# In two graph passes, a third of the table look-ups is replaced by GpSimd gathers weighed on ScalarE

## The chip, the cores and the metric

The kernel runs on one core of a Trainium2 chip. The metric is the device time of one execution, in microseconds (us). Engines are called TensorE (PE in the profile, its weight loads PEld), VectorE (DVE), ScalarE (ACT), GpSimd (POOL) and SyncE (SP, which here only issues transfers).

## The reference, cut to what matters

A graph of 3125 nodes (64 values each) and 100000 edges passes through four layers. The change touches the last, a signed graph convolution that is applied twice. With weights split by sign, each application is a sum over edges:

```
wp, wn = where(w >= 0, w, 0), where(w < 0, -w, 0)
def gcn(x, w):                     # for wp and for wn, with a weight matrix and bias each
    dinv = rsqrt(segment_sum(w, dst) + 1)
    agg  = segment_sum((x @ W.T)[src] * (dinv[src] * w * dinv[dst]), dst)
    return agg + (x @ W.T) * dinv**2 + b
h   = relu(gcn(x, wp) - gcn(x, wn))
out = relu(gcn(h, wp) - gcn(h, wn))
```

So for each edge a row of its source node is taken, multiplied by the edge's two weights (positive and negative part, 64 values each, 128 in all), and added to its target node.

## The kernel before, in words

Nodes are kept in 25 tiles (`NT`) of 125 nodes, one node per partition. Edges have been sorted into slots of 128: 36 bins of target nodes, three bins (`SLOTS = 3`) handled at a time, for each of the 25 source tiles. One source tile with its three bins is a chunk; there are 12 x 25 = 300 chunks (`NCHUNK`), in an order that is fixed in the program. Edges that find no slot are "left over" and are done in a loop behind each pass.

`edge_pass` is called three times: for "edges" (an earlier layer), "near" and "far" (the two applications of the signed convolution, line tags `sp_` and `sq_`). In near and far, chunk c goes like this:

- SyncE loads `hot_src` (a 128 x 384 one-hot matrix, three slots of 128 columns, bf16) from DRAM into a ring of eight buffers (`load_hot`, line 2292).
- TensorE looks up the source rows (`look_up`, line 1599): for each of three slots, three matmuls with the one-hot slot as weights and the node table as moving operand. The table is split into three bf16 pieces, so that the sum is exact in f32; it has 66 columns in near (64 values and two scales) and 128 in far. Nine matmuls fill one PSUM bank. Look-ups run three chunks ahead (`LOOK_AHEAD`).
- VectorE makes `hot_dst` (line 1417, here "the target": which row of a bin each edge goes to, 128 x 270), in near multiplies the two looked-up scales with the edge weights (`weigh`, line 1425, "the weights"), and multiplies the looked-up rows by them into `msg` (line 1450, "the message", 128 x 384).
- TensorE sums messages by target (`add_up`, line 1611): three f32 matmuls, 90 x 128 each, which the trace shows as six weight loads and six matmuls. They accumulate over 25 chunks.
- ScalarE copies the sums out once in 25 chunks (`evacuate`, line 1557), and SyncE stores the result.

Every step waits on semaphores that count chunks (`rows_taken`, `dst_made`, `looked_up`, `added`), so that an engine runs ahead by the number of its buffers: four for messages and targets, six PSUM banks for look-ups. At the start of near, ScalarE also computes `k.table` = x times the two scales (`far_terms`, line 2536, 50 activations), which is used only behind the pass. GpSimd issues one gather of left-over rows per pass (line 1382) and then waits.

An earlier pass, `relation_pass` (`rp_`), already takes the third slot of most chunks by a GpSimd gather (line 1783) in place of a look-up.

Of the kernel before, what the change touches and what calls it, by code (L numbers as in the profile page):

```python
# [14 lines left out]
P = 128  # L15
# [156 lines left out]
class Program:  # L172
    def __init__(self, nc, ctx, dram):
# [41 lines left out]
        self.near_rows = dram_rows("near_rows", NPAD, D + 2)  # L215
        self.far_rows = dram_rows("far_rows", NPAD, H)
        self.hot_rows = nc.dram_tensor("hot_rows", (NCHUNK, P, SLOTS * P), BF16, kind="Internal").ap()

# [1031 lines left out]


def edge_pass(k, tag, kind, pieces, table, width, cols, sem, ring, aside=None, act_aside=None):

# [9 lines left out]
    DST_SLOTS, MSG_SLOTS, SUM_SLOTS, HOT_SLOTS = 4, 4, 3, Ring.HOT_SLOTS  # L1263
    edges = kind == "edges"
    KEY_BANKS = 2 if edges else 0
    ROW_BANKS = 6 - KEY_BANKS
    slots = lambda a, c: a[:, c * SLOTS:(c + 1) * SLOTS]
    with ExitStack() as ctx:
# [6 lines left out]
        fence, weighed, squared = sem("fence"), sem("weighed"), sem("squared")  # L1275
        hot_io, hot_src = ring.hot_io, ring.hot_src

        found = FIELD if edges else width
# [40 lines left out]
        with nc.Block() as block:  # L1319
# [56 lines left out]
            @block.gpsimd  # L1376
            def _(pool):
                if aside:
                    aside(nc.gpsimd)
                ring.wait_rows(pool)  # L1380
                pool.wait_ge(left_idx, 1)
                pool.indirect_dma_start(left_row[:, :], None, table,
                                        bass.IndirectOffsetOnAxis(left_no[:, 0:1], 0)).then_inc(left_rows, 16)
                left_count = pool.value_load(k.left_tiles[0:1, 0:1], min_val=1, max_val=EPAD // P)
                with pool.Fori(0, left_count) as i:
                    pool.wait_ge(left_idx, i + 2)
                    pool.sem_inc(fence, 1)
                    pool.indirect_dma_start(left_row[:, :], None, table,
                                            bass.IndirectOffsetOnAxis(left_no[:, 0:1], 0)).then_inc(left_rows, 16)
                    pool.wait_ge(left_rows, i * 16 + 32)  # L1390
                    pool.sem_inc(fence, 1)

            @block.vector
            def _(dve):
# [26 lines left out]
                def weigh(c):  # L1421
                    got = looked(c)
                    if c >= MSG_SLOTS:
                        dve.wait_ge(rows_taken, c - MSG_SLOTS + 1)
                    v.tensor_tensor(factor[:, c % MSG_SLOTS, :, :], got[:, :, D:D + 2], slots(k.slot_w, c), ALU.mult)\
                        .then_inc(weighed, 1)
# [5 lines left out]
                def message(c):  # L1432
# [15 lines left out]
                    else:  # L1448
                        by, x = slots(k.slot_w, c), got.rearrange("p s (a f) -> p s a f", a=2)
                    v.tensor_tensor(to, x, by.unsqueeze(3).broadcast_to([P, SLOTS, 2, D]), ALU.mult)\  # L1450
                        .then_inc(rows_taken, 1)

# [77 lines left out]
            def _(act):  # L1530
# [22 lines left out]
                def evacuate(j):  # L1553
# [3 lines left out]
                    nc.scalar.activation(totals[:, j % 2, :, :], sum_bank(j), ACT.Copy).then_inc(evacuated, 1)  # L1557

                nc.scalar.preload_act_table(ACT.Copy)
                if act_aside:  # L1560
                    act_aside(nc.scalar)
                for c in range(-SPELL_AHEAD, NCHUNK):
                    ahead = c + SPELL_AHEAD - 1
                    if edges and c >= 0:
                        rectify(c)
                    if edges and 0 <= ahead < NCHUNK:
                        square_key(ahead)
                    if edges and 0 <= ahead - 1 < NCHUNK:
                        hot_source(ahead - 1)
                    if c % NT == 1 and c > NT:  # L1570
                        evacuate(c // NT - 1)
# [6 lines left out]
            def _(pe):  # L1578
# [10 lines left out]
                def look_up(c):  # L1589
# [5 lines left out]
                    if c >= ROW_BANKS:  # L1595
                        pe.wait_ge(rows_taken, c - ROW_BANKS + 1)
                    for s in range(SLOTS):
                        for piece in range(3):
# [5 lines left out]
                def add_up(c):  # L1604
                    j, i = c // NT, c % NT
                    pe.wait_ge(dst_made, c + 1)
                    pe.wait_ge(msg_made if edges else rows_taken, c + 1)
                    if i == 0 and j >= 2:
                        pe.wait_ge(evacuated, j - 1)
# [890 lines left out]
def program(nc, dram, out):  # L2500
    with ExitStack() as ctx:
# [27 lines left out]
        with nc.sbuf_tensor("near_pieces", [P, NT, 3, D + 2], BF16) as pieces, ExitStack() as held, semaphores(nc, "sp") as sem:  # L2529
            ring = Ring(k, held, sem, "sp")  # L2530
            near_table(k, pieces, sem, ring)

            def far_terms(act):
                for t in range(NT):
                    for j in range(2):
                        act.activation(k.table[:, t, j * D:(j + 1) * D], k.x[:, t, :], ACT.Copy, scale=k.dinv[:, t, j:j + 1])

            edge_pass(k, "sp", "near", pieces, k.near_rows, D + 2, H, sem, ring, act_aside=far_terms)
        with nc.sbuf_tensor("far_pieces", [P, NT, 3, H], BF16) as pieces, ExitStack() as held, semaphores(nc, "sq") as sem:
            ring = Ring(k, held, sem, "sq")  # L2540
            gcn_mid(k, pieces, sem, ring)
# [58 lines left out]
```

## Time and profile before

| | us |
|---|---|
| median of 3 runs | 3882.38 |
| lowest and highest run | 3877.11, 3891.0 |
| profiled execution, its time | 3880.98 |
| profiled execution, span from first to last instruction | 3879.3 |
| near, first look-up to last message | 3102.9 to 3399.7 |
| far, first look-up to last message | 3462.6 to 3816.7 |

Over the span TensorE is busy 75%, VectorE 77%, ScalarE 36%, GpSimd 31%. These shares are means over stages with different limits; the two passes that the change touches are to be read from their own stretches.

### The profile page before, as it was taken

The numbers are of one execution on the slowest core, as the hardware profiler recorded it, in microseconds if no ns is written. First come the engines' busy times: TensorE is split into PE (matmuls) and PEld (weight loads), VectorE is DVE, ScalarE is ACT, GpSimd is POOL, SyncE is SP. The second block draws the span as 40 slices with busy tenths as digits, with TensorE's granted clock in tenths as the row PEclk, the third lists the DMA queues.
The fourth block names the chain that finished last, engine by engine and source line by source line (L and its number), as shares of the span: only waits on it lengthen the run. The fifth ranks groups of instructions, "written<-read, shape, count | busy, mean of one in ns | idle before, by whom it ended". The sixth has DMA issues, their size and how long they took to land. (4 is left out here: it accounts for less than half of the span.)

```text
span 3879.3 us, 77817 instructions
## 1 busy us (share of the span) xinstructions
PE 2903.3 (75%) x25843; PEld 2103.0 (54%) x25926; DVE 2985.1 (77%) x6871; ACT 1393.6 (36%) x2725; POOL 1210.0 (31%) x1109
## 2 busy tenths in 40 slices
PE   0158888888407707707769999699999699979994
PEld 0135555555302202202259999456565499969994
DVE  6877777778589999999977777555555599968887
ACT  0024444444304405405459999233333210010000
POOL 0034445455238737636600000155555100000000
PEclk9998888889659959959979999799999799989997
DMA  7936565556458828728847675122222144323331
GB/s 304 378 98 179 147 182 163 166 161 182 148 162 289 260 83 283 253 88 277 258 157 219 216 230 168 47 66 69 66 65 66 37 107 108 106 55 89 91 90 37
DMA packets 444431, 596.30 MB, mean 154 GB/s; under 512 B 82795, under 2 KB 331434, under 8 KB 444052
## 3 DMA queue, kind: packets, MB, share of 16 engines
q1 hardware_dynamic: 395623, 450.37, 39.4%
q0 software_dynamic: 34592, 68.90, 5.9%
q10 hardware_dynamic: 13836, 72.12, 4.8%
q8 instruction: 220, 3.60, 0.4%
q14 instruction: 160, 1.30, 0.1%
HBM read 354.68 MB, written 230.75 MB: 151 GB/s over the span
## 5 line engine op out<-in xcount | busy, mean ns | idle before, releaser
L1213 PE MATMUL psum<-a_probs,z 128*65 128x512 f32 (+1 forms) x1050 | 436.3, 555 | 134.1 <-DVE a_probs L1111 133.4
L914 POOL DMA_INDIRECT slots<-bc_rec,idx x400 | 392.1, 980 | 399.8 <-ACT bc_rec L874 300.8
L1806 DVE TENSOR_SCALAR rp_hot_dst<-rp_ramp,slot_key 128x696 bf16<-128x696 f16 x900 | 298.8, 401 | 230.3 <-PE psum L1950 230.3
L535 POOL DMA_INDIRECT slots<-h,idx x256 | 336.7, 1315 | 310.8 <-DMA h<-recs 239.8
L1147 ACT ACTIVATE a_tops<-a_tops,a_s_low 128x512 f32<-128x512 f32 (+2 forms) x300 | 283.0, 946 | 271.8 <-DVE a_tops L1102 254.7
L1213 PEld LDWEIGHTS psum<-a_probs,z 128*65 128x65 f32 x1050 | 122.5, 139 | 443.5 <-DVE a_probs L1111 275.3
L1783 POOL DMA_INDIRECT rp_fetch<-piece_rows,slot_row x283 | 279.2, 987 | 247.5 <-PE psum L1950 191.1
L1102 DVE SCALAR_TENSOR_TENSOR a_tops<-table,a_s_rest,big 128x512 f32<-128x512 f32 (+2 forms) x300 | 307.7, 1028 | 2.8 <-DMA big<-shift_rows 2.8
L1111 DVE SCALAR_TENSOR_TENSOR a_probs<-a_tops,a_counts 128x512 f32<-128x512 f32 (+2 forms) x300 | 289.8, 967 | 11.4 <-ACT a_tops L1147 7.6
L1878 ACT ACTIVATE rp_msg<-psum 128x192 bf16<-128x192 f32 (+1 forms) x456 | 176.2, 387 | 310.3 <-PE psum L1924 275.6
L793 PE MATMUL psum<-acc 128*128 128x512 f16 x1000 | 194.1, 339 | 115.3 <-issue 64.2
L1611 PE MATMUL psum<-sp_msg,sp_hot_dst 128*90 128x128 f32 x1800 | 260.2, 281 | 0.0
L1611 PE MATMUL psum<-ep_msg,ep_hot_dst 128*90 128x131 f32 x1800 | 257.2, 278 | 3.3 <-ACT ep_msg L1535 3.1
L1611 PE MATMUL psum<-sq_msg,sq_hot_dst 128*90 128x128 f32 x1800 | 252.2, 277 | 0.0
L762 DVE TENSOR_SCALAR acc<-bc_ramp,bc_key_s,bc_base_s 128x625 f16<-128x625 f16 x500 | 245.9, 492 | 6.0 <-issue 6.0
L1941 PE MATMUL psum<-rp_hot_dst,rp_msg 128*128 128x184 bf16 (+1 forms) x1151 | 239.9, 307 | 10.2 <-DVE rp_hot_dst L1806 2.0
L1204 PE MATMUL psum<-ident,a_shifts 128*10 128x128 f32 x15 | 5.7, 377 | 283.6 <-DVE a_shifts L1096 266.3
L1599 PE MATMUL psum<-edge_pieces,ep_hot_src 128*128 128x131 bf16 x2700 | 209.8, 222 | 0.8 <-ACT ep_hot_src L1550 0.7
L1438 DVE TENSOR_TENSOR ep_sums<-psum,ep_rec 128x393 f32<-128x393 f32 x300 | 169.8, 566 | 52.5 <-PE psum L1599 49.8
L1611 PEld LDWEIGHTS psum<-ep_msg,ep_hot_dst 128*90 128x90 f32 x1800 | 206.6, 158 | 5.8 <-DVE ep_hot_dst L1417 5.7
L1599 PE MATMUL psum<-far_pieces,sq_hot_src 128*128 128x128 bf16 x2700 | 200.7, 220 | 5.2 <-PEq L2077 5.2
L1611 PEld LDWEIGHTS psum<-sp_msg,sp_hot_dst 128*90 128x90 f32 x1800 | 203.1, 159 | 0.0
(452 smaller groups left out, 6613.7 us busy)
## 6 DMA issues: line engine op xcount, KB each, us to landing
slots<-big ACTq DMA_DIRECT2D x60, 1012.5 KB
ep_rec<-slots SPq DMA_DIRECT2D x60, 1012.5 KB, 6.0
a_counts<-edge_counts SPq DMA_DIRECT2D x75, 538.5 KB
a_counts<-edge_counts SPq DMA_DIRECT2D x150, 256.0 KB
a_counts<-edge_counts SPq DMA_DIRECT2D x75, 512.0 KB
edge_counts<-bc_counts SPq DMA_DIRECT2D x12, 3125.0 KB
hot_rows<-ep_hot_src SPq DMA_DIRECT2D x300, 96.0 KB
sp_hot_src<-hot_rows SPq DMA_DIRECT2D x300, 96.0 KB
```

Of the source, the lines that this page charges most:

```text
L535: pool.indirect_dma_start(k.slots, bass.IndirectOffsetOnAxis(k.idx[:, at:at + 1], 0), self.rows[y][:, t, :], None).then_inc(self.scattered ...
L762: last = v.tensor_scalar(to_s[:, u, :], ramp[:, :], column(key_s, t), column(base_s, j), ALU.subtract, ALU.is_equal)
L914: pool.indirect_dma_start(k.slots, bass.IndirectOffsetOnAxis(k.idx[:, first + t:first + t + 1], 0), rec[:, j, t, :], None).then_inc(scatte ...
L1102: v.scalar_tensor_tensor(tops[:, cols], shift_1[:, cols], s_rest[:, s:s + 1], shift_2[:, cols], ALU.add, ALU.max).then_inc(topped, 1)
L1111: v.scalar_tensor_tensor(probs[:, cols], tops[:, cols], 1.0, counts[:, cols], ALU.min, ALU.mult)\
L1147: nc.scalar.activation(tops[:, cols], tops[:, cols], ACT.Exp, bias=s_low[:, s:s + 1])\
L1213: last = nc.tensor.matmul(sums[:, a:b], k.z[:, s, 0:D + 1], probs[:, a:b], start=s == 0, stop=True, skip_group_check=True)
L1599: last = nc.tensor.matmul(got[:, s, :], hot_src[:, c % HOT_SLOTS, s * P:(s + 1) * P], pieces[:, c % NT, piece, :], start=s == 0 and piece ...
L1611: last = nc.tensor.matmul(sum_bank(j)[:, s, :], hot_dst[:, c % DST_SLOTS, s, :], msg[:, c % MSG_SLOTS, s, :], start=i == 0 and s == 0, sto ...
L1783: pool.indirect_dma_start(fetch[:, n % FETCH_SLOTS, :], None, k.piece_rows, bass.IndirectOffsetOnAxis(k.slot_row[:, c:c + 1], 0))\
L1806: v.tensor_scalar(hot_dst[:, q % HOT_SLOTS, :], ramp[:, :], k.slot_key[:, q:q + 1], None, ALU.is_equal)\
L1941: nc.tensor.matmul(sum_bank(s, part), message(q)[:, 0:2 * D], hot_dst[:, q % HOT_SLOTS, a:b], start=starts_bank(q, part), stop=True, skip_ ...
```

## The change

In near and far, chunks with c % 3 other than 2 (from chunk 25 on in near, from 5 on in far: 183 and 196 of 300) are handled differently in their third slot:

- TensorE looks up two slots, not three (six matmuls), and only 256 of the 384 one-hot columns are loaded.
- GpSimd gathers the 128 source rows of the third slot from DRAM by an indirect transfer, 128 f32 values (512 bytes) each, into a ring of six buffers (`fetch`); a buffer is free when ScalarE has used it. In far the rows come from the table in DRAM that is there already (`far_rows`). In near they come from a new one, `term_rows`: a copy of `k.table`, which ScalarE stores once its 50 activations are done, and GpSimd waits for.
- ScalarE multiplies the gathered rows by the edge's two weights, in two activations of 128 x 64, straight into the third slot of `msg`.
- VectorE weighs two slots, not three; the target keeps all three.
- TensorE waits for ScalarE's products (`fetch_taken`) before it sums a fetched chunk.

```diff
+def edge_fetches(kind):
+    first = {"edges": NCHUNK, "near": NT, "far": FIRST_FETCH}[kind]
+    return [c for c in range(first, NCHUNK) if c % 3 != 2]
+
+def looked_columns(kind):
+    return lambda c: (SLOTS - 1 if c in edge_fetches(kind) else SLOTS) * P
...
+    FETCHES = edge_fetches(kind)
+    FETCH_NO, FETCH_SLOTS = {c: n for n, c in enumerate(FETCHES)}, 6
+    looked_slots = lambda c: SLOTS - 1 if c in FETCH_NO else SLOTS
...
             def _(pool):
...
+                if kind == "near":
+                    pool.wait_ge(terms_in, 16)
+                for n, c in enumerate(FETCHES):
+                    if n >= FETCH_SLOTS:
+                        pool.wait_ge(fetch_taken, n - FETCH_SLOTS + 1)
+                    pool.indirect_dma_start(fetch[:, n % FETCH_SLOTS, :], None, k.term_rows if kind == "near" else table,
+                                            bass.IndirectOffsetOnAxis(k.slot_row[:, c:c + 1], 0))\
+                        .then_inc(fetch_in[n % FETCH_SLOTS], 16)
...
-                    v.tensor_tensor(to, x, by.unsqueeze(3).broadcast_to([P, SLOTS, 2, D]), ALU.mult)\
-                        .then_inc(rows_taken, 1)
+                    some = slice(0, looked_slots(c))
+                    v.tensor_tensor(to[:, some], x[:, some], by[:, some].unsqueeze(3).broadcast_to([P, looked_slots(c), 2, D]),
+                                    ALU.mult).then_inc(rows_taken, 1)
...
+                def weigh_fetched(c):
+                    n = FETCH_NO[c]
+                    act.wait_ge(fetch_in[n % FETCH_SLOTS], 16 * (n // FETCH_SLOTS + 1))
+                    if c >= MSG_SLOTS:
+                        act.wait_ge(added, c - MSG_SLOTS + 1)
+                    at = c * SLOTS + SLOTS - 1
+                    for j in range(2):
+                        last = nc.scalar.activation(msg[:, c % MSG_SLOTS, SLOTS - 1, j * D:(j + 1) * D],
+                                                    fetch[:, n % FETCH_SLOTS, j * D:(j + 1) * D], ACT.Copy,
+                                                    scale=k.slot_w[:, at, j:j + 1])
+                    last.then_inc(fetch_taken, 1)
...
                 if act_aside:
-                    act_aside(nc.scalar)
+                    act_aside(nc.scalar).then_inc(terms_made, 1)
+                    act.wait_ge(terms_made, 1)
+                    act.dma_start(k.term_rows.rearrange("(t p) f -> p t f", p=P), k.table[:, :, :]).then_inc(terms_in, 16)
                 for c in range(-SPELL_AHEAD, NCHUNK):
+                    if c in FETCH_NO:
+                        weigh_fetched(c)
...
-                    for s in range(SLOTS):
+                    for s in range(looked_slots(c)):
                         for piece in range(3):
...
                     pe.wait_ge(msg_made if edges else rows_taken, c + 1)
+                    if c in FETCH_NO:
+                        pe.wait_ge(fetch_taken, FETCH_NO[c] + 1)
```

## Rows read from the trace of the kernel before

**Rows 1.** Windows: busy us of PE, PEld, DVE, ACT, POOL; PE clock; DMA share; GB/s
```profile
3200.00:3250.00 50.00, 50.00 (x766) 49.41 (x764) 50.00 (x152) 0.97 (x2) 0.00 (x0) 1.00 0.40 108
...
3600.00:3650.00 50.00, 50.00 (x637) 49.52 (x636) 42.34 (x85) 0.97 (x2) 0.00 (x0) 1.00 0.31 85
```

**Rows 2.** Timeline of near: start, duration (us), engine, line, output, inputs
```profile
3252.40 0.43 PEld L1599 LDWEIGHTS psum<-near_pieces,sp_hot_src 128*128 128x128 bf16 x9
...
3252.59 0.43 DVE L1417 TENSOR_TENSOR sp_hot_dst<-bin_lane,slot_dst 128x270 f32<-128x270 f32 x1
3252.76 0.67 PEld L1611 LDWEIGHTS psum<-sp_msg,sp_hot_dst 128*90 128x90 f32 x6
...
3252.99 0.17 DVE L1425 TENSOR_TENSOR sp_factor<-psum,slot_w 128x6 f32<-128x6 f32 x1
3253.10 0.56 DVE L1450 TENSOR_TENSOR sp_msg<-psum,sp_factor 128x384 f32<-128x384 f32 x1
3253.39 0.43 PEld L1599 LDWEIGHTS psum<-near_pieces,sp_hot_src 128*128 128x128 bf16 x9
```

**Rows 3.** Timeline of far, one chunk of TensorE's weight loads
```profile
3602.54 0.60 PEld L1599 LDWEIGHTS psum<-far_pieces,sq_hot_src 128*128 128x128 bf16 x9
...
3603.10 0.67 PEld L1611 LDWEIGHTS psum<-sq_msg,sq_hot_dst 128*90 128x90 f32 x6
...
3603.72 0.60 PEld L1599 LDWEIGHTS psum<-far_pieces,sq_hot_src 128*128 128x128 bf16 x9
```

**Rows 4.** Windows of 10 ns of the weight loads alone, near, then far
```profile
3252.50:3252.51 0.01, 0.00 (x1) 1.00 0.00 0
...
3602.64:3602.65 0.01, 0.00 (x0) 1.00 1.18 384
```

**Rows 5.** Timeline of the first chunks of near
```profile
3103.72 0.43 DVE L1417 TENSOR_TENSOR sp_hot_dst<-bin_lane,slot_dst 128x270 f32<-128x270 f32 x1
3103.89 1.09 POOL L1382 DMA_INDIRECT sp_left_row<-near_rows,sp_left_no  x1 [37.17 <-DVE sp_left_no L1454]
...
3106.69 0.43 DVE L1417 TENSOR_TENSOR sp_hot_dst<-bin_lane,slot_dst 128x270 f32<-128x270 f32 x1
...
3107.04 0.16 DVE L1425 TENSOR_TENSOR sp_factor<-psum,slot_w 128x6 f32<-128x6 f32 x1
3107.11 0.55 DVE L1450 TENSOR_TENSOR sp_msg<-psum,sp_factor 128x384 f32<-128x384 f32 x1
3107.58 0.43 DVE L1417 TENSOR_TENSOR sp_hot_dst<-bin_lane,slot_dst 128x270 f32<-128x270 f32 x1
```

**Rows 6.** Timeline of ScalarE at the start of near
```profile
3104.20 12.04 ACT L2536 ACTIVATE table<-x,dinv 128x64 f32<-128x64 f32 x50
3130.60 0.49 ACT L1557 ACTIVATE sp_totals<-psum 90x384 f32<-90x384 f32 x1 [14.35 <-PE psum L1611]
```

**Rows 7.** Timeline of GpSimd in the relation pass
```profile
2602.40 0.98 POOL L1783 DMA_INDIRECT rp_fetch<-piece_rows,slot_row  x1 [0.30 <-issue]
```

**Rows 8.** Timeline of the attention stage, GpSimd and VectorE
```profile
1217.45 2.08 POOL L535 DMA_INDIRECT slots<-h,idx  x1 [0.30 <-issue]
1217.46 1.21 DVE L1111 SCALAR_TENSOR_TENSOR a_probs<-a_tops,a_counts 128x1024 f32<-128x1024 f32 x1
...
1218.60 0.74 DVE L1102 SCALAR_TENSOR_TENSOR a_tops<-table,a_s_rest,big 128x512 f32<-128x512 f32 x1
...
1219.83 0.97 POOL L535 DMA_INDIRECT slots<-h,idx  x1 [0.30 <-issue]
1219.86 1.27 DVE L1102 SCALAR_TENSOR_TENSOR a_tops<-table,a_s_rest,big 128x1024 f32<-128x1024 f32 x1
```

**Rows 9.** Timeline of a left-over gather behind near
```profile
3411.18 0.95 POOL L1388 DMA_INDIRECT sp_left_row<-near_rows,sp_left_no  x1 [306.20 <-DVE sp_left_no L1454]
...
3413.87 0.15 DVE L1476 TENSOR_TENSOR sp_left_out<-sp_left_row,sp_left_rec 128x2 f32<-128x2 f32 x1
```

**Rows 10.** Window behind the far table's last store, columns as in rows 1
```profile
3458.00:3462.00 4.00, 0.00 (x0) 0.00 (x0) 3.86 (x6) 2.21 (x3) 0.00 (x0) 0.61 0.31 82
```

More of the change, by code:

```diff
@@ L216, in __init__ @@
         self.far_rows = dram_rows("far_rows", NPAD, H)
+        self.term_rows = dram_rows("term_rows", NPAD, H)
         self.hot_rows = nc.dram_tensor("hot_rows", (NCHUNK, P, SLOTS * P), BF16, kind="Internal").ap()
@@ L1276, in edge_pass @@
         hot_io, hot_src = ring.hot_io, ring.hot_src
+        if FETCHES:
+            fetch, fetch_in = sb("fetch", [P, FETCH_SLOTS, H]), [sem(f"fetch_in{y}") for y in range(FETCH_SLOTS)]
+            fetch_taken, terms_made, terms_in = sem("fetch_taken"), sem("terms_made"), sem("terms_in")
         found = FIELD if edges else width
@@ L1424, in weigh @@
                         dve.wait_ge(rows_taken, c - MSG_SLOTS + 1)
-                    v.tensor_tensor(factor[:, c % MSG_SLOTS, :, :], got[:, :, D:D + 2], slots(k.slot_w, c), ALU.mult)\
+                    some = slice(0, looked_slots(c))
+                    v.tensor_tensor(factor[:, c % MSG_SLOTS, some, :], got[:, some, D:D + 2], slots(k.slot_w, c)[:, some], ALU.mult)\
                         .then_inc(weighed, 1)
@@ L1449, in message @@
                         by, x = slots(k.slot_w, c), got.rearrange("p s (a f) -> p s a f", a=2)
-                    v.tensor_tensor(to, x, by.unsqueeze(3).broadcast_to([P, SLOTS, 2, D]), ALU.mult)\
-                        .then_inc(rows_taken, 1)
+                    some = slice(0, looked_slots(c))
+                    v.tensor_tensor(to[:, some], x[:, some], by[:, some].unsqueeze(3).broadcast_to([P, looked_slots(c), 2, D]),
+                                    ALU.mult).then_inc(rows_taken, 1)
                 def left_number():
@@ L2529, in program @@
         with nc.sbuf_tensor("near_pieces", [P, NT, 3, D + 2], BF16) as pieces, ExitStack() as held, semaphores(nc, "sp") as sem:
-            ring = Ring(k, held, sem, "sp")
+            ring = Ring(k, held, sem, "sp", hot_cols=looked_columns("near"))
             near_table(k, pieces, sem, ring)
@@ L2535, in far_terms @@
                     for j in range(2):
-                        act.activation(k.table[:, t, j * D:(j + 1) * D], k.x[:, t, :], ACT.Copy, scale=k.dinv[:, t, j:j + 1])
+                        last = act.activation(k.table[:, t, j * D:(j + 1) * D], k.x[:, t, :], ACT.Copy,
+                                              scale=k.dinv[:, t, j:j + 1])
+                return last
             edge_pass(k, "sp", "near", pieces, k.near_rows, D + 2, H, sem, ring, act_aside=far_terms)
         with nc.sbuf_tensor("far_pieces", [P, NT, 3, H], BF16) as pieces, ExitStack() as held, semaphores(nc, "sq") as sem:
-            ring = Ring(k, held, sem, "sq")
+            ring = Ring(k, held, sem, "sq", hot_cols=looked_columns("far"))
             gcn_mid(k, pieces, sem, ring)
```

## The prediction

> **What bounds the kernel now.** I read the busy time by stretches first, to see how the two edge passes that the diff touches (near and far) are filled; then the timeline inside three chunks of each, because a busy share does not say who waits for whom; then the places of the trace where GpSimd issues indirect transfers, since the change puts 379 of them beside other work.
>
> In both passes TensorE is busy for the whole 50 us, ScalarE for 1 us and GpSimd not at all [rows 1]; the granted clock is 1.00 (2.4 GHz). In near VectorE looks as full as TensorE. The timeline decides between the two. One chunk of near takes 0.99 us (first weight load of the look-ups at 3252.40, the next chunk's at 3253.39), of which 0.36 us go to the nine look-ups and 0.63 us to the six weight loads of the three f32 sums [rows 2]. Those six start evenly (0.67 us long, last load 0.16: five steps of 0.10 us), so TensorE does not pause among them. VectorE does pause: where nothing holds it, its steps are 0.35 us from target to weights, 0.07 to the message and 0.47 to the next target, 0.89 us in all [rows 5]; in the steady state the first step is 0.40 us and the second 0.11 [rows 2], since the weights wait for the look-up. So near is bound by TensorE with VectorE about 0.1 us behind it. In far a chunk takes 1.18 us, 0.56 of it look-ups and 0.62 sums [rows 3], with VectorE idle for 15% of the stretch [rows 1].
>
> **One look-up.** The first weight load after the f32 sums has a gap of its own: in near loads begin at 3252.40 and then at 3252.51, in far at 3602.54 and 3602.65 [rows 2 to 4]. That 0.11 us is paid once per chunk and stays. The other eight of near end with the last load's start at 3252.40+0.43-0.10 = 3252.73: seven steps in 0.22 us, 0.031 us each. Far: 3602.54+0.60-0.10 = 3603.04, seven steps in 0.39 us, 0.056 us each. These I take. Bounds: the whole stretch over nine (0.040 and 0.062, as if the gap shrank too), and nothing, if a shorter batch only leaves TensorE waiting.
>
> **What is removed.** Fetched chunks are those from 25 (near) or 5 (far) on with c % 3 other than 2: 183 and 196. Each loses three of nine look-ups. Near: 183 x 3 x 0.031 = 17.0 us. Far: 196 x 3 x 0.056 = 32.9 us. VectorE's message shrinks from 384 to 256 columns; its step of 0.47 us against the target's 0.35 for 270 columns gives about 1.05 ns a column, so 0.13 us less, and 0.76 us a chunk against TensorE's new 0.90 in near: it stays behind, and this edit is worth nothing by itself (without the removed look-ups it would be worth nothing too). The loads of SP stay 300 a pass; two thirds of them carry 64 KB in place of 96. The DMA share is 0.40 in near and 0.31 in far [rows 1], and a fetch adds 64 KB where 32 KB went: hidden while the eight-deep ring of loads holds.
>
> **What is added on ScalarE.** Two 128x64 activations with a per-node scale for each fetched chunk: the same form is there 50 times in 12.04 us, 0.24 us each [rows 6], so 0.48 us against a chunk of 0.90. It may start when the sums of chunk c-4 are done, some three chunks (2.7 us) ahead of its use. Cost 0 while that lead holds, 0.48 us a chunk if it is gone. Queued behind a waiting activation is the evacuation of the sums, 0.49 us [rows 6]; SP's placing of the totals waits for that, and TensorE only two groups of 25 chunks later.
>
> **What is added on TensorE.** One more wait in the summing of fetched chunks. Before the sums it waits twice now, and the first f32 load follows the last look-up load by 0.03 us (3252.73 to 3252.76) [rows 2], so a wait that is long met costs nothing visible. I take 0; above, see the last rival.
>
> **What is added on GpSimd.** One gather of 128 rows per fetched chunk. The relation pass issues the same kind in 0.98 us with 0.30 us between two [rows 7]: 1.28 us a fetch, 2.56 for two. Behind the fetches on its queue stand only the gathers of left-over edges, which come after the pass; ahead of them one such gather and, in near, the wait for the new table. Three chunks, two of them fetched, take 0.90+0.90+0.99 = 2.79 us of TensorE in near (2.97 before) and 3.21 in far. So far has 0.6 us to spare for two fetches and near 0.23.
>
> That small margin is where near is decided. In the attention stage a gather or scatter that GpSimd begins just as VectorE runs a two-input f32 operation lasts 2.08 us in place of 0.97: begun at 1217.45, it ends at 1219.53, which is 0.97 after 1218.56, just before VectorE's next operation starts at 1218.60 [rows 8]. The one gather that stands beside the target operation of near itself shows the same on a small scale: begun 0.17 us into that operation, it lasts 1.09 us [rows 5], so it was held some 0.12 us, until 0.29 us after the target's start. The target is a two-input f32 operation; it would hold a fetch by 0 to 0.30 us. No hold per pair: two fetches in 2.56 us, TensorE sets the pace, near gains 17.0. One full hold: 2.86 us, near gains 91.5 x (2.97-2.86) = 10.1. Two full holds: 3.16 us, near loses 91.5 x 0.19 = 17.4. A fetch that is held starts right behind a target, and 1.28 us later it is past the next target (0.90 us on), so holds come about once in a pair: I take the middle of the first two, 13.5 us. In far even two holds (3.16 us) stay under TensorE's 3.21: 32.9 us stand.
>
> Conversely VectorE could be held by GpSimd. In rows 8 a gather starts at 1219.83 and VectorE begins a 1024-column operation at 1219.86 that lasts 1.27 us, while the gather runs its 0.97; the same width took 1.21 at 1217.46. I charge nothing: 0.06 us is inside VectorE's slack.
>
> The Trainium skill, page "SBUF — State Buffer", section "SBUF: two separate sides", says that VectorE and GpSimd share one port pair by an exclusive lock, taken by a two-input VectorE operation against a GpSimd one that reads SBUF, whoever starts first holding it for the whole instruction while the other fully blocks. By that rule a fetch would also hold the target for up to 0.97 us. For GpSimd's side the trace agrees (2.08 against 0.97 us), for VectorE's it does not (1.27 against 1.21 us). What such a lock would do here is the second rival.
>
> **Start of near.** The fetches wait for a new store of 25 x 64 KB, issued by ScalarE once its 50 activations end at 3116.24 [rows 6]. The far table's last store, a fifth as large, keeps the 16 transfer engines busy for 0.31 of 4 us, 1.24 us, [rows 10], so the whole takes 6.2 us alone, 10.3 in the 0.60 that the loads leave [rows 1]; with some 2 us of way, 3125 to 3129. A gather's row is used at most 2.7 us after its start [rows 9], and ScalarE adds 0.5: ready at 3128 to 3132. The first fetched chunk is summed right after the group whose evacuation starts at 3130.60 [rows 6]. So 0 to 1.4 us of stall, 8 if the store takes twice as long; I take 1. In far GpSimd is free from the start and the first fetch is for chunk 6, over 7 us in: nothing.
>
> **Sum.** 13.5 - 1 + 32.9 = 45.4 us off the profiled execution's 3880.98: 3835.6. The median of the three runs lies 1.4 above that execution: 3837.
>
> **The rivals.**
> 1. GpSimd becomes the bound of near: every fetch is held for the full 0.30 us. Near +17.4, far -32.9, start 1: -14.5, so 3868. For it: the attention stage shows runs of alternately held scatters. Against: two targets are 0.90 us apart, and a held fetch frees the next.
> 2. The lock works both ways: a target cannot run inside a fetch. Three chunks then need two fetches (1.96 us) and three targets (1.05) one after another, 3.01 us: near +3.7 against 2.97, far still 3.21: -28, so 3854. Against: the 1.27 us of rows 8.
> 3. It ends slower: ScalarE's products come late, so that TensorE waits in each fetched chunk. It decides at 45.4 / 379 = 0.12 us a fetched chunk; with one of the two activations exposed (0.24 us) it is 379 x 0.24 = 91 us, so 3882 + 91 - 45 = 3928. For it: near's fetches may never get ahead. Against: 2.7 us of lead, and far's margin of 0.6 us a pair.
> 4. The removed look-ups do not shorten a chunk, because another wait already ends there (VectorE's weights in near, the target's release in far): about 3882. Against: the even steps of rows 2 and 3.
>
> **Chances.** Forecast 0.60 (own range 3824 to 3850, from 0.040/0.062 per look-up to near gaining nothing), rival 1 0.12, rival 2 0.13, rival 3 0.08, rival 4 0.07. Range 3824 to 3868: it leaves out rivals 3 and 4 and a little of rival 1. About 0.3% (11.6 us) can be told from no change. Faster: forecast, rival 2 and some two thirds of rival 1, 0.81; same: rival 4 and the rest of rival 1, 0.11; slower: 0.08.
>
> **What would show it.** Right: in far three chunks every 3.21 us, six look-ups in a fetched chunk, TensorE without a pause; in near three chunks in 2.79 to 2.86 us, fetches of 0.97 to 1.28 us. Wrong: targets that last over 0.45 us (rival 2), GpSimd without idle time but its 0.30 us and sums that wait for ScalarE in near (rival 1), such waits in far (rival 3), an unchanged 0.99 or 1.18 us (rival 4). A lower granted clock after waits of TensorE would break the sum too.

## The result and the profile after

The changed kernel takes 3965.68 us (median of 4 runs, 3954.02 to 3974.0) against 3879.74 before: ratio 1.0226, 95% interval 1.0194 to 1.0257. The prediction was 3837, so the sign is wrong. Two views of the changed kernel say where the time is; first the windows, one of near and one of far, columns as in [rows 1]:

```profile
3200.00:3250.00 50.00, 42.65 (x533) 40.84 (x531) 34.27 (x120) 15.42 (x55) 27.77 (x28) 0.93 0.40 104
3600.00:3650.00 50.00, 47.04 (x551) 44.76 (x549) 32.53 (x86) 17.07 (x60) 27.72 (x29) 1.00 0.40 105
```

Then the look-ups (first two rows) and sums (last two) of near and of far by tile; the last numbers ahead of the forms are the starts of the first and the last matmul (us):

```profile
L1643 PE MATMUL psum<-near_pieces,sp_hot_src x2151: 190/193/262, 3108.4 to 3472.2; 128*128 128x66 bf16 x196
...
L1643 PE MATMUL psum<-far_pieces,sq_hot_src x2112: 216/219/314, 3543.2 to 3899.2; 128*128 128x128 bf16 x192
...
L1657 PE MATMUL psum<-sp_msg,sp_hot_dst x1800: 272/273/501, 3110.4 to 3474.8; 128*90 128x128 f32 x180
...
L1657 PE MATMUL psum<-sq_msg,sq_hot_dst x1800: 269/273/466, 3547.0 to 3901.8; 128*90 128x128 f32 x180
```

In the kernel before, the same rows run from 3102.9 to 3400.7 and from 3462.6 to 3818.4. So near went from 297.8 to 366.4 us and far from 355.8 to 358.6. From near's end to far's first look-up it is 68.4 us in place of 61.9, from far's end to the end of the span 68.4 in place of 60.9. With 5.5 us ahead of near, in stages that the change does not touch, this is the whole difference of the spans (3970.2 - 3879.3 = 90.9).

The windows also give the rate. Three near chunks are now 6+6, 6+6 and 9+6 matmuls, 39; 533 in 50 us is 3.66 us for three, where before 766 of 45 each gave 2.94 [rows 1]. In near TensorE is busy for 7 us less of 50 than before, VectorE for 16 less, and GpSimd for 28 of 50. No engine is busy throughout: they wait for each other. The granted clock of this stretch is 0.93 where it was 1.00; that is not the cause, since the first experiment loses as much at 1.00.

The waits of near, 3160 to 3460 (us in total, times, longest):

```profile
ACT sp_msg L1594 <- PE psum L1657: 158.7, 75, 3.6
POOL sp_fetch L1407 <- ACT sp_msg L1594: 100.7, 61, 3.2
DVE sp_factor L1452 <- PE psum L1643: 63.1, 64, 2.2
PEld psum L1657 <- issue: 52.7, 79, 1.7
...
PE psum L1657 <- issue: 35.6, 54, 1.6
...
PE psum L1657 <- DVE sp_msg L1478: 8.8, 20, 0.8
```

GpSimd waits for ScalarE, ScalarE for sums, VectorE for look-ups; and TensorE waits for "issue", which means for nothing that the profile shows, and by the profile hardly for VectorE. The first gathers of near show how that can be. The timeline, without weight loads:

```profile
3129.29 0.44 PE L1643 MATMUL psum<-near_pieces,sp_hot_src 128*128 128x66 bf16 x9
...
3129.76 0.17 DVE L1452 TENSOR_TENSOR sp_factor<-psum,slot_w 128x6 f32<-128x6 f32 x1
3129.81 0.95 POOL L1407 DMA_INDIRECT sp_fetch<-term_rows,slot_row  x1 [19.38 <-DMA term_rows<-table]
...
3130.27 0.45 PE L1643 MATMUL psum<-near_pieces,sp_hot_src 128*128 128x66 bf16 x9
...
3131.07 0.95 POOL L1407 DMA_INDIRECT sp_fetch<-term_rows,slot_row  x1 [0.30 <-issue]
3131.26 0.45 PE L1643 MATMUL psum<-near_pieces,sp_hot_src 128*128 128x66 bf16 x9
3131.54 0.86 PE L1657 MATMUL psum<-sp_msg,sp_hot_dst 128*90 128x128 f32 x6
3131.89 0.17 DVE L1452 TENSOR_TENSOR sp_factor<-psum,slot_w 128x6 f32<-128x6 f32 x1 [1.12 <-PE psum L1643]
...
3132.71 0.86 PE L1657 MATMUL psum<-sp_msg,sp_hot_dst 128*90 128x128 f32 x6
3133.41 0.32 PE L1643 MATMUL psum<-near_pieces,sp_hot_src 128*128 128x66 bf16 x5
...
3135.56 0.17 DVE L1452 TENSOR_TENSOR sp_factor<-psum,slot_w 128x6 f32<-128x6 f32 x1 [2.65 <-PE psum L1643]
...
3136.10 0.95 POOL L1407 DMA_INDIRECT sp_fetch<-term_rows,slot_row  x1 [0.30 <-issue]
...
3137.68 0.19 PE L1643 MATMUL psum<-near_pieces,sp_hot_src 128*128 128x66 bf16 x1 [0.42 <-issue]
3138.41 0.29 PE L1643 MATMUL psum<-near_pieces,sp_hot_src 128*128 128x66 bf16 x4 [0.54 <-issue]
3138.51 0.59 ACT L1594 ACTIVATE sp_msg<-sp_fetch,slot_w 128x64 f32<-128x64 f32 x2 [16.80 <-PE psum L1657]
```

Counted in order, the look-ups of 3129.29, 3130.27 and 3131.26 are those of chunks 22, 23 and 24. VectorE's weights need nothing newer than the look-up of their chunk. Those of chunk 22 start at 3129.76, 0.03 us after it ended; those of chunk 23 at 3131.89, 1.2 us after, with TensorE already two groups of matmuls on; those of chunk 24 at 3135.56, 3.9 us after it ended at 3131.71. Six gathers, each 1.26 us behind the last, fill 3129.81 to 3137.05; once they are over, ScalarE and VectorE go on at 3138.51. TensorE itself falls apart into matmuls that come singly. No product of ScalarE exists yet: its first is that of 3138.51. So work that TensorE has done is not known to the engines that wait for it, while GpSimd issues gathers.

The starts of TensorE's matmuls part the loss in two. Inside a group (the look-ups of a chunk, or its sums) the program has no wait, and in the steady state of the kernel before no matmul there starts more than 0.16 us after the one ahead of it. In 300 us of near (3150 to 3450) the first sum of a chunk starts 0.27 us (mean) after the matmul ahead of it, where it was 0.03: 59 us more in 244 chunks. Of these starts 79 are more than 0.15 us behind, and each of the 79 comes at most 0.15 us after VectorE's message of its chunk ends, which is its last input in all 79; ScalarE's product is so in none. So TensorE does wait for VectorE there, and VectorE for word of the look-ups. Nine pauses of over 0.35 us inside groups make 7 us more. In far (3580 to 3880) it is the other way round: the first sums start nearly as before (0.065 against 0.056 us), and 34 pauses inside groups make 23.7 us. So near loses mainly because other engines learn late, far mainly because TensorE itself stops.

The trace of before had this too, in a stage that the prediction didn't read, the sorting of the edges, where GpSimd issues scatters back to back:

```profile
402.04 1.16 PE L803 MATMUL psum<-w_W1a_edge,h 64*128 64x128 f32 x8
402.04 0.97 POOL L914 DMA_INDIRECT slots<-bc_rec,idx  x1 [0.30 <-issue]
...
404.65 0.21 PE L793 MATMUL psum<-acc 128*128 128x113 f16 x1 [0.18 <-issue]
...
406.82 0.21 PE L793 MATMUL psum<-acc 128*128 128x113 f16 x1 [1.06 <-issue]
407.15 0.97 POOL L914 DMA_INDIRECT slots<-bc_rec,idx  x1 [0.30 <-issue]
...
409.90 0.71 ACT L859 ACTIVATE bc_counts<-psum 128x625 f32<-128x625 f32 x1 [7.63 <-DMA tile_ranges<-ek_ends]
410.18 0.25 DVE L761 TENSOR_SCALAR bc_more_t<-bc_ramp,bc_key_t 128x128 f16<-128x128 f16 x1 [5.22 <-remote]
```

Line 859 waits for a counter that TensorE raises with the first matmul of line 803, at 402.04. It starts at 409.90, 7.9 us later and behind the last of eight scatters (398.21 to 408.12), and TensorE's matmuls come singly meanwhile. The names in the brackets mislead: the profile puts a wait down to what it can find.

### The profile page after: what moved, and what is told of

Its sections match the earlier page's. It is cut to its first block and busy times, and to the rows that moved or that the text cites. A ratio compares the mean times of both kernels' runs of the same rounds, so it can differ in the third digit from the quotient of the medians.

```text
span 3970.2 us, 77072 instructions
## 1 busy us (share of the span) xinstructions
PE 2889.1 (73%) x24706; PEld 2070.7 (52%) x24789; DVE 2880.7 (73%) x6871; ACT 1601.0 (40%) x3483; POOL 1592.1 (40%) x1488
## 5 line engine op out<-in xcount | busy, mean ns | idle before, releaser
L1407 POOL DMA_INDIRECT sq_fetch<-far_rows,slot_row x196 | 195.5, 997 | 152.2 <-ACT sq_msg L1594 109.3
L1407 POOL DMA_INDIRECT sp_fetch<-term_rows,slot_row x183 | 184.3, 1007 | 169.8 <-ACT sp_msg L1594 108.8
L1657 PEld LDWEIGHTS psum<-sq_msg,sq_hot_dst 128*90 128x90 f32 x1800 | 204.9, 159 | 14.4 <-issue 13.9
```

The lines of the kernel that those rows point to most:

```text
L1407: pool.indirect_dma_start(fetch[:, n % FETCH_SLOTS, :], None, k.term_rows if kind == "near" else table, bass.IndirectOffsetOnAxis(k.slot_r ...
L1657: last = nc.tensor.matmul(sum_bank(j)[:, s, :], hot_dst[:, c % DST_SLOTS, s, :], msg[:, c % MSG_SLOTS, s, :], start=i == 0 and s == 0, sto ...
```

## The experiments

Three theories. **A:** while GpSimd issues an indirect transfer, TensorE's semaphore increments reach the other engines late, whoever uses the rows. **B:** ScalarE's products come late and TensorE waits for them (rival 3 of the prediction). **C:** TensorE's third wait holds its queue. All ratios are to the kernel before on the same chip, with 95% intervals.

**Gathers without use.** All slots are looked up again; a wait of ScalarE for its own work six fetches back is added.

```
-    looked_slots = lambda c: SLOTS - 1 if c in FETCH_NO else SLOTS
+    looked_slots = lambda c: SLOTS
-        last = nc.scalar.activation(msg[:, c % MSG_SLOTS, SLOTS - 1, ...
+        last = nc.scalar.activation(spare[:, n % FETCH_SLOTS, ...
-                    if c in FETCH_NO:
-                        pe.wait_ge(fetch_taken, FETCH_NO[c] + 1)
```

> The changed kernel with its gathers kept and their use taken out: all three slots of a chunk are looked up again and weighed by VectorE, ScalarE weighs the fetched rows into a tile that nothing reads, and TensorE's wait for them is gone; the pace of the gathers (six ahead, released by ScalarE, which starts from the sums of TensorE) stays. Theory A (while GpSimd issues a gather, TensorE's semaphore increments reach the other engines late, whoever uses the rows): the passes lose as in the changed kernel or more, since every chunk costs 0.99 or 1.18 us again: 3,940 us or more, ratio to before 1.015 or above. Theory B (ScalarE's products come late and TensorE waits for them, the slower rival of the prediction): no product is waited for, so about 3,880, ratio 0.997 to 1.003.

Measured: 3963.03 us, ratio 1.0258 (1.0204 to 1.0313). The whole loss against the kernel before is there although nobody uses a fetched row: A, not B or C. Most of it is in near, which takes 366.3 us (366.4 in the changed kernel); far takes 368.2. The windows of near and far, where before had x766 and x637:

```profile
3200.00:3250.00 50.00, 42.77 (x614) 40.71 (x613) 38.63 (x125) 16.08 (x58) 26.37 (x27) 1.00 0.44 118
3600.00:3650.00 50.00, 49.69 (x629) 48.80 (x628) 36.54 (x86) 16.30 (x58) 28.05 (x29) 1.00 0.49 132
```

By the starts of the sums of chunks 60 and 270, three chunks take 3.68 us in near and 3.62 in far here, with all look-ups, and 3.69 and 3.56 in the changed kernel, with fewer. So in these two passes a pair of gathers takes some 3.6 us, 1.8 each, whatever TensorE has to look up.

**Six gathers a pass, everything else as changed.**

```
+                    if n >= FETCH_SLOTS:
+                        pool.sem_inc(went, 1)
+                        continue
                     pool.indirect_dma_start(fetch[:, n % FETCH_SLOTS, :], ...
```

> The changed kernel with six gathers in each pass in place of 183 and 196: after the first six, GpSimd only counts a semaphore up by one where the gather stood, and ScalarE weighs the six old rows again and again, so the sums are not those of the graph. Every wait between ScalarE, TensorE and VectorE stays as in the changed kernel. Theory A: without gathers the increments come at once, and the passes cost what the prediction worked out: 3,825 to 3,850 us, ratio 0.986 to 0.993. Theory B: the products are as late as before, since ScalarE starts from the same increments: 3,930 or more. Theory C: 3,950 to 3,980.

Measured: 3834.27 us, ratio 0.9918 (0.9889 to 0.9947).

```profile
3200.00:3250.00 50.00, 50.00 (x706) 49.39 (x705) 47.90 (x163) 21.94 (x75) 0.00 (x0) 1.00 0.34 89
3600.00:3650.00 50.00, 50.00 (x611) 49.49 (x609) 39.90 (x94) 18.89 (x64) 0.00 (x0) 1.00 0.31 81
```

TensorE is full again, and 39 matmuls take 2.76 and 3.19 us. By the starts of the sums of chunks 60 and 270 three chunks take 2.784 and 3.210 us: the prediction said 2.79 and 3.21. ScalarE's part and the third wait cost nothing in the steady state.

**The third wait moved to VectorE.**

```
+                    if c in FETCH_NO:
+                        dve.wait_ge(fetch_taken, FETCH_NO[c] + 1)
...
-                    if c in FETCH_NO:
-                        pe.wait_ge(fetch_taken, FETCH_NO[c] + 1)
```

> The changed kernel with TensorE's third wait moved: VectorE waits for ScalarE's product ahead of its own message, so that TensorE's wait for VectorE covers both, and TensorE has the two waits of the kernel before. Theory A: the gathers stand, so 3,950 to 3,990 us. Theory C: TensorE's queue is free again, 3,830 to 3,860. Theory B: the product is as late and only another engine waits for it, 3,950 to 4,000.

Measured: 3946.4 us, ratio 1.0221 (1.0177 to 1.0264). Against C; a little below A's range of times, the same ratio as the changed kernel's.

**Which part of a gather?** Two kernels on the base of the first: GpSimd works but issues nothing, or the same bytes move but GpSimd does not issue them.

```
-                    pool.indirect_dma_start(fetch[:, n % FETCH_SLOTS, :], None, ...
+                    nc.gpsimd.iota(busy[:, n % FETCH_SLOTS, :], pattern=[[1, 1000]], ...).then_inc(went, 1)
```

> As the kernel with unused gathers, but GpSimd writes a ramp of 1,000 numbers (about 0.9 us by the 2.9 us that 3,200 take in the kernel before) where it issued a gather; ScalarE weighs rows that lie in the core's memory, and nothing reads the result. The waits and the pace are the same. If the gathers hold TensorE's increments because GpSimd issues transfers (theory A, issue): 3,865 to 3,895 us. If any work of GpSimd does it: 3,940 or more. Theory B: 3,880.

```
+                    act.dma_start(fetch[:, n % FETCH_SLOTS, :], source[first:first + P, :])
```

> As the kernel with unused gathers, but the transfers (the same 128 rows of 512 bytes into the same places, at consecutive addresses) are issued from ScalarE's queue as plain loads, and GpSimd issues none. If it is GpSimd's issuing that holds TensorE's increments (theory A, issue): 3,865 to 3,895 us, and GpSimd's long last instruction at the end of the pass is gone too. If it is the transfers on the DMA engines, beside SyncE's loads: 3,940 or more.

Measured: 3878.93 us, ratio 1.0006 (0.9985 to 1.0027), and 3884.86 us, ratio 1.0017 (0.9993 to 1.0041). Neither GpSimd's work nor the transfers' traffic does it. The window of the second, in which the engines for transfers are busier (0.55 against 0.40) and TensorE is full:

```profile
3200.00:3250.00 50.00, 50.00 (x764) 49.41 (x761) 50.00 (x153) 20.80 (x70) 0.00 (x0) 1.00 0.55 152
```

The addresses are consecutive here and GpSimd's were scattered, so it is GpSimd's issuing of indirect transfers that is shown; a plain transfer issued by GpSimd was not tried. The Trainium skill, page "DMA: Bandwidth & Descriptors", section "SWDGE vs HWDGE vs iDMA", says that GpSimd writes the descriptors of its transfers into rings in SBUF, and that transfers issued by SyncE or ScalarE never touch this path. That fits the pair of runs; what of it reaches TensorE's increments, no run here shows.

**Longer leads.** If increments are late, a longer lead should hide it.

```
+    if not edges:
+        LOOK_AHEAD, DST_SLOTS, MSG_SLOTS = 5, 8, 8
```

> The changed kernel with longer leads in the two signed passes: TensorE looks up five chunks ahead in place of three, and the rings of targets and of messages have eight places in place of four. Theory A: a late increment costs nothing as long as the lead covers it; most of the near stalls are 1 to 2.5 us, the lead grows by two chunks (some 1.8 us) for the look-ups and four (some 3.6 us) for the sums, so most of the loss comes back: 3,840 to 3,890 us. Theory B: ScalarE may weigh eight chunks ahead, so this recovers too, 3,835 to 3,860. Theory C: the third wait stands, 3,950 to 3,980.

Then ScalarE alone gets a longer lead, by a ring of its own for the third slots:

```
-                    if c >= MSG_SLOTS:
-                        act.wait_ge(added, c - MSG_SLOTS + 1)
+                    if n >= THIRD_SLOTS:
+                        act.wait_ge(added, FETCHES[n - THIRD_SLOTS] + 1)
```

> The changed kernel with a ring of its own for the weighed third slots, eight of them, which is twelve chunks: ScalarE may weigh twelve chunks ahead in place of four; VectorE's messages, targets and look-ups keep their leads. Theory A: the increments are as late as before for VectorE and SyncE, whose leads are the same: 3,940 to 3,985 us. Theory B: the products are there long before TensorE wants them: 3,835 to 3,860.

Measured: 4004.23 us, ratio 1.0359 (1.0318 to 1.0401), and 4091.85 us, ratio 1.0584 (1.0543 to 1.0625). Every expectation failed, A's too, and B is refuted for six gathers ahead: products that may come twelve chunks early make it worse. The starts of the sums show the manner: 15 near chunks took, one group after another, 18.7, 22.4, 14.7, 19.8, 16.0 and 21.8 us with longer leads (14.8 us in nearly every group of the kernel before), and 14.4 to 27.1 us with the ring of third slots. Stretches at full speed alternate with held ones. With longer leads the first sums of near start nearly on time (0.057 us after the matmul ahead of them), but 68 pauses inside groups make 52 us in 300 (3130 to 3430): the lead hides the late increments, as A said, and TensorE itself stops instead, which A had not said. In near, 79 of the changed kernel's gathers follow the last within 1.4 us, 104 with longer leads, 121 with the ring: the more chunks ScalarE may work ahead, the longer the runs of gathers that GpSimd is let into. The leads alone, on the kernel before:

> The kernel before, without any gather of the change, with the longer leads alone (look-ups five chunks ahead, eight places for targets and messages). Theory A: no gathers, so TensorE's increments come at once and the leads are not used: 3,870 to 3,890 us, ratio 0.997 to 1.003. If longer leads are bad in themselves, as they were beside the gathers (40 us with two chunks of three, 26 us with one of three): 3,895 or more.

Measured: 3879.57 us, ratio 0.999 (0.9966 to 1.0013). They are harmless without gathers. Shorter runs should then help:

```
-    FETCH_NO, FETCH_SLOTS = {c: n for n, c in enumerate(FETCHES)}, 6
+    FETCH_NO, FETCH_SLOTS = {c: n for n, c in enumerate(FETCHES)}, 2
```

> The changed kernel with two gathers ahead in place of six, so that GpSimd can issue at most two back to back before ScalarE has to free a place. Theory A: the longer lead of the kernel with five chunks ahead made the time longer because its increments, once free, let loose a longer run of gathers; with runs of two the longest delay is about 2.7 us and the time comes down, to 3,890 to 3,945 us. Theory B: the fetched rows have less lead, so the products come later still: 3,966 or more.

Measured: 3969.06 us, ratio 1.0283 (1.0237 to 1.0329). It did not, and this time lies where B had put it (3,966 or more). The starts of the passes recovered (chunks 15 to 30 of near took 15.0 us in place of 22.2), and the pauses inside groups are gone (none over 0.35 us in 300 us of either pass), with 41 gathers of near within 1.4 us of the last. The rest did not recover: 3.76 us for three chunks in near, 3.83 in far. The waits of near, 3130 to 3430, show a new bound:

```profile
ACT sp_msg L1594 <- DMA sp_fetch<-term_rows,slot_row: 194.8, 147, 3.6
...
PE psum L1657 <- ACT sp_msg L1594: 42.7, 64, 2.2
```

ScalarE now waits for rows, and TensorE for ScalarE: of 100 first sums of near that start more than 0.15 us behind the matmul ahead of them (3115 to 3415), 99 come right after ScalarE's product, where it was VectorE's message in the changed kernel. From a gather's start to ScalarE's it takes 2.67 us (median, near), the two activations take 0.59, and the gather that reuses the buffer starts 0.27 us later: with two buffers, two gathers need 3.53 us, where three chunks should take 2.79 and 3.21. So at this share a lead of two gathers is too short by itself, and the run does not say what short runs of gathers would be worth.

**Fewer gathers.** One chunk in three is fetched:

```
-    return [c for c in range(first, NCHUNK) if c % 3 != 2]
+    return [c for c in range(first, NCHUNK) if c % 3 == 0]
```

> The changed kernel with one chunk of three fetched in place of two, so that a gather comes every 2.9 us or so and not every 1.4: 91 and 99 look-ups of a slot fewer, 8.5 and 16.6 us by the prediction's rates. Theory A: TensorE's increments are held for some 1.4 us after a gather starts and are free until the next one, so a look-up is 1.4 us late at most and the lead of two chunks hides it or nearly: 3,850 to 3,885 us. Theory B: the product of a fetched chunk is as late as in the changed kernel, half as often: 3,910 to 3,930.

Measured: 3874.77 us, ratio 1.0002 (0.9974 to 1.0029). The steady state is better than A had expected:

```profile
3200.00:3250.00 50.00, 50.00 (x738) 49.39 (x737) 46.58 (x158) 11.42 (x38) 16.39 (x18) 1.00 0.45 121
3600.00:3650.00 50.00, 50.00 (x622) 49.49 (x621) 41.17 (x89) 9.67 (x32) 14.49 (x15) 1.00 0.36 99
```

TensorE is full. From chunk 60 to 270 three chunks take 2.880 and 3.377 us, against 2.962 and 3.545 before; one fetched chunk in three should give 0.093 and 0.168, so 2.869 and 3.377. Here gathers cost next to nothing. What ate the gain lies at the ends. At the start of far six gathers are issued back to back: its first 15 chunks took 21.3 us against 17.7, and chunks 15 to 30 of near 20.7 against 14.8. And at the end of a pass GpSimd drains, with all engines waiting. Its drains at the three edge passes' ends (ns, min/median/max; the first pass has few gathers), of before, then of the changed kernel, then of this one:

```profile
L1319 POOLq DRAIN  x3: 306/306/311, 2449.4 to 3842.5; - x3
```

```profile
L1337 POOLq DRAIN  x3: 311/6358/7416, 2453.2 to 3926.2; - x3
```

```profile
L1337 POOLq DRAIN  x3: 306/7742/8314, 2446.3 to 3832.2; - x3
```

6.4 and 7.4 us in the changed kernel, where the stretches behind the two passes had grown by 6.5 and 7.5.

**The drain moved, then the share and the run of gathers tuned.** GpSimd drains right behind a pass's last gather, beside the last chunks:

```
+                if FETCHES:
+                    pool.drain()
                 left_count = pool.value_load(...)
```

> The kernel with one chunk of three fetched, with one instruction more: GpSimd drains right after the last gather of a pass, beside the last chunks, and not only at the end of the pass, where its drain took 7.7 and 8.3 us with all engines waiting. If the length of the drain comes from the gathers behind it, the one at the end falls under 1 us and both passes' ends give back some 14 us: 3,855 to 3,865 us against 3,871 of before. If the drain is long whenever GpSimd gathered in a pass, no change from 3,875.

Measured: 3869.42 us, ratio 0.9967 (0.9944 to 0.999); by the ratio 12.8 us below before, whose median was 3878.71 beside it. With longer leads as well:

> One chunk of three fetched, the early drain, and the longer leads (look-ups five chunks ahead, eight places for targets and messages). Theory A: with gathers 2.9 us apart an increment is 1.4 us late at most, which the longer lead covers, so the passes come down to the rates of the kernel with few gathers: near and far 8 and 16 us below before, 3,840 to 3,855 us with the drains hidden. If longer leads are bad in themselves, as with all gathers, where they made the time 40 us longer: 3,870 or more.

Measured: 3895.81 us, ratio 1.003 (1.0006 to 1.0055): A's forecast failed again, the leads are bad beside gathers even at this share. In its profile the drains (8.8 and 9.4 us) lie beside the last chunks and the stretches behind the passes are back at 62.0 and 61.0 us. With one far chunk in two fetched, and the short leads:

```
+    return [c for c in range(first, NCHUNK) if c % (2 if kind == "far" else 3) == 0]
```

> The early drain, one chunk of three fetched in the near pass as in the kernel with the early drain, and one chunk of two in the far pass: 147 gathers there, one every 2.2 us or so. By the prediction's rate 24.7 us of look-ups go. If each gather costs the far pass what it cost at 98 gathers (16.5 us of look-ups gone, 11.9 us measured, so 0.05 us a gather), the far pass gains 17 us and the whole some 19 us: 3,855 to 3,863 us where before takes about 3,878. Theory A has the loss rise faster than the number of gathers, since the free time between two of them falls from about 2 us to 0.8 us: no better than the kernel with one chunk of three and the early drain, 3,865 to 3,880 us.

Measured: 3864.5 us, ratio 0.9939 (0.9916 to 0.9962); the time is in neither range, with a median of 3887.35 for the kernel before beside it. Theory A's version was wrong here: far took 3.294 us for three chunks, just what one and a half look-ups of a slot fewer should give (3.545 - 1.5 x 0.168 = 3.293). Then two gathers ahead in place of six, and one near chunk in two as well:

> One chunk of three fetched in the near pass, one of two in the far pass, the early drain, and two gathers ahead in place of six. By the trace of the kernel with the same share of gathers the steady rates are those of the prediction (2.88 us for three near chunks), and the loss sits in chunks 15 to 30 of near (21.6 us for 15 chunks against 14.8 of before) and in the first 15 of far (23.2 against 17.7), where six gathers are issued back to back. Theory A: with two at most back to back these stretches fall to the steady rate, some 6 us in each pass: 3,848 to 3,858 us where before takes 3,880. If the start of a pass is slow for another reason (the term store, the first rows), no change: 3,860 to 3,868.

> One chunk of two fetched in both signed passes, the early drain, two gathers ahead. In near a gather then comes every 1.9 us. If the increments are free from about 1.4 us after a gather's start until the next one, half a microsecond is left for the three or four increments of two chunks, and near keeps a gain of 46 more look-ups of 0.093 us a chunk, 4 us below the kernel with one of three: 3,845 to 3,854. If the free time is too short, near stalls as it did with two of three and the whole is 3,870 or more.

Measured: 3852.88 us, ratio 0.9939 (0.9917 to 0.9962), and 3860.37 us, ratio 0.9964 (0.9941 to 0.9986). The first is in A's range, the second in neither. In the first, the starts came down as A said: the window from 2.8 us after far's first look-up, with six ahead,

```profile
3470.00:3495.00 25.00, 22.59 (x231) 20.90 (x230) 15.13 (x35) 4.11 (x14) 11.41 (x13) 0.86 0.35 91
```

and with two:

```profile
3453.00:3478.00 25.00, 25.00 (x297) 24.71 (x296) 19.27 (x45) 5.28 (x18) 10.43 (x11) 0.95 0.39 103
```

231 matmuls against 297; part of it may be the granted clock (0.86 against 0.95). In the profiles near fell from 298.2 to 290.1 us and far from 337.6 to 332.3 (first look-up to last sum's start), though the two ratios can't be told apart. In the second, near stalled again (TensorE 48.26 of 50 us): 3.09 us for three chunks, where 2.82 were due. Of its first sums of 3125 to 3375, 44 start more than 0.15 us behind the matmul ahead of them; the last input is VectorE's message for 42 and ScalarE's product for two, so that here it is late increments again and hardly the two buffers. So both kernels with 0.9939 beat the kernel before, by 0.6%, and the changed one; two ahead, one near chunk in three, one far chunk in two is the one to keep, though what two ahead add to it is seen in the stretches alone.

## Why the prediction was wrong

**The look-ups: right.** 0.031 and 0.056 us each; with six gathers a pass three chunks took 2.784 and 3.210 us where it said 2.79 and 3.21.

**ScalarE and TensorE's third wait at nothing: right** in the steady state, by the same run. Rival 3 had the sign but not the mechanism: ScalarE does wait for sums, 158.7 us of 300, because it learns of them late, yet its product is the last input of none of the 79 late sums above, and the loss stays when no product is used.

**GpSimd: the step that failed.** It asked what a gather costs GpSimd (1.28 us) and whether VectorE's port holds it, and took the rest of the engines as untouched. The held port was hardly there: gathers of near take 0.95 us (median; 1.20 at most), 133 targets that begin inside a gather take 0.42 to 0.47 us, and GpSimd is busy for 28 us of 50 (rivals 1 and 2 fall). What a gather costs is TensorE's word to the others and, beside runs of gathers, TensorE's own pauses. Of the trace's records of TensorE's two counters in near (3150 to 3450), none falls 1.15 to 1.35 us behind a gather's start, in 269 chances of 0.1 us; 1.65 to 1.75 us behind it, where no new gather has begun, 52 fall in 67 chances. With a gather every 1.4 us, as two in the prediction's 2.79 us would have it, hardly any time is left. Near became 68.6 us longer where 12.5 were to be won, and far lost all of its 32.9 and 2.8 more.

Rows 7 were read for their duration only. The relation pass, from which they are, would not have shown the loss: with 28 gathers in 50 us, as many as near has now, TensorE is busy there for 49.56.

```profile
2700.00:2750.00 50.00, 49.56 (x443) 30.13 (x448) 28.26 (x86) 19.13 (x49) 27.19 (x28) 1.00 0.28 68
```

So a price that holds in one pass was carried to another with other chunks; why the relation pass bears it, no run here shows. The scatters shown above had the sign, and what other engines did beside them was not read.

**The start of near at 1 us, far's at nothing: too small.** Even with only six gathers a pass, near's chunks 15 to 30 took 20.9 us against 14.8 before, and far's first 15 took 21.3 against 17.7. With two ahead, one chunk in three fetched, near's took 14.7, so it is the six gathers back to back.

**GpSimd's queue behind the fetches: a term was missing,** GpSimd's drain at the end of a pass: 13.8 us for the two passes where it was 0.6.

**Loads, VectorE's message:** hidden, as said; with few gathers TensorE is full in both passes.

## What to carry to other kernels

Price an indirect transfer of GpSimd not by its own duration but by what the other engines wait for meanwhile: look in the trace for a stage that already has them back to back, see whether TensorE's consumers start late there, and then measure it in the pass that is to have them. In these two passes gathers that took GpSimd 1.28 us each came every 1.8 us with two chunks in three fetched, and TensorE with them. They were nearly free in the steady state where the chunks left 2.2 us or more for each, with the short leads (one far chunk in two, one near in three); one near chunk in two, with 1.9 us for each, took 2.1 and lost. Keep gathers spaced and out of bursts, but with buffers enough for a row's way (2.67 us here), and let GpSimd drain while others work. A longer lead does not hide such a delay if it also lets the cause run faster.

## What was not expected of the hardware

TensorE's increments reach the others late while GpSimd issues indirect transfers (3.9 us for VectorE's weights after the look-up of chunk 24; 7.9 us for line 859 beside scatters), and beside runs of gathers TensorE itself pauses inside a group, for up to 1.5 us in far, where the program has no wait. GpSimd's drain took 3.9 to 9.4 us behind 91 to 196 gathers of a pass, 0.8 behind six and 0.3 without, and was not longer for more gathers (8.8 behind 91, 4.5 behind 147). Left open: by which path a gather reaches TensorE's increments, whether the pauses have the same cause, why the relation pass bears as many gathers, and what sets the length of the drain.
